# Graph kernel on one core: the third relation's degrees later in the query product, the last product in three fp32r passes

## What is computed

```python
# first layer (three relations): messages are averaged per relation
out = x @ W_root + bias
for r in range(3):
    m = etype == r
    s = segment_sum(where(m, msg, 0), dst); c = segment_sum(m, dst)
    out = out + s / maximum(c, 1.0)[:, None]
# and the gate's query part, one row for each of 8 x 64 queries
qg = einsum('blf,gf->blg', q, Wg[:, F:]) + bg
# last layer (34 relations, then a graph convolution)
mean = agg.reshape(34, n, -1) / maximum(cnt, 1.0)
h1 = einsum('rni,rio->no', mean, W_rel) + x @ W_root + b_rgcn
xw = h1 @ W_gcn                                   # the last product
out = segment_sum(xw[src] * norm[:, None], dst) + xw * (dinv * dinv)[:, None] + b_gcn
```

## Time and profile before

| | us |
|---|---|
| median of 3 runs | 1069.91 |
| lowest, highest | 1068.56, 1072.1 |
| the profiled execution | 1069.65 |
| its span | 1067.8 |
| TensorE busy | 1029.7 |
| VectorE busy | 767.6 |
| ScalarE busy | 574.3 |
| GpSimd busy | 263.5 |

### The profile page before, as it was taken

The page is one execution under the profiler, slowest core; times in us unless marked ns, Lnnn a source line. Parts: engine busy times, 40 slices in busy tenths (PEclk is TensorE's granted clock), DMA queues, the critical chain, the costliest instruction groups (busy, mean ns, idle before and its releaser), DMA issues.

```text
span 1067.8 us, 17748 instructions
## 1 busy us (share of the span) xinstructions
PE 1029.7 (96%) x7444; PEld 853.1 (80%) x7444; DVE 767.6 (72%) x1106; ACT 574.3 (54%) x612; POOL 263.5 (25%) x166
## 2 busy tenths in 40 slices
PE   8999999999999999999899989999999999999997
PEld 6799986454689984445869879967999999999994
DVE  7993855888754237888654495755989898989873
ACT  0433216888633338888324373424767676767650
POOL 3524704899400027988100000000000000000000
PEclk9999999999999999999999999999999999999999
DMA  8033247221042374221335302614978787878740
GB/s 302 12 126 142 90 144 233 63 66 55 6 178 89 119 231 144 60 60 41 109 129 187 125 1 90 214 49 155 302 254 281 256 279 254 280 256 279 255 168 32
DMA packets 82324, 163.20 MB, mean 153 GB/s; under 512 B 4076, under 2 KB 60168, under 8 KB 81950
## 3 DMA queue, kind: packets, MB, share of 16 engines
q1 hardware_dynamic: 80768, 151.86, 42.0%
q0 software_dynamic: 1472, 10.15, 3.4%
HBM read 158.35 MB, written 0.80 MB: 149 GB/s over the span
## 4 chain that ended last, share of the span: by engine, by line
PE 81%; DVE 11%; issue 3%; ACT 2%; DMA 1%; POOL 0%; SPq 0%; DVEq 0%; ACTq 0%
PE PS L1139 20%; PE PS L803 8%; PE PS L974 7%; PE PS L819 6%; PE PS L602 5%; PE PS L701 5%; PE PS L1122 5%; PE PS L725 4%; PE PS L532 4%; PE PS L621 3%; PE PS L545 3%; PE PS L1155 2%; PE PS L1041 2%; DVE PRD L1756 2%; PE PS L861 2%
## 5 line engine op out<-in xcount | busy, mean ns | idle before, releaser
L2025 DVE TENSOR_TENSOR Wlo<-W,Whi 128x2304 fp32r<-128x2304 f32 x68 | 172.1, 2550 | 18.9 <-ACT Whi L1496 18.9
L1496 ACT CAST Whi<-W 128x2304 fp32r<-128x2304 f32 x68 | 144.4, 2126 | 0.0
L1139 PE MATMUL PS<-Whi,Mhi 128*128 128x384 f32 x408 | 138.1, 338 | 0.0
L1139 PE MATMUL PS<-Wlo,Mhi 128*128 128x384 f32 x408 | 136.6, 335 | 0.0
L1139 PE MATMUL PS<-Whi,Mlo 128*128 128x384 f32 x408 | 136.5, 335 | 0.0
L499 POOL TENSOR_TENSOR PRDP<-arena 128x1024 f32<-128x1024 f32 x48 | 114.7, 2390 | 33.0 <-issue 20.6
L803 PE MATMUL PS<-QH,SEL 128*128 128x512 f32 x384 | 115.8, 422 | 5.9 <-DVE PRD L1756 1.5
L1338 ACT ACTIVATE arena<-PS 128x1024 f32<-128x1024 f32 x96 | 98.5, 1026 | 24.2 <-PE PS L803 24.2
L803 PEld LDWEIGHTS PS<-QH,SEL 128*128 128x128 f32 x384 | 64.8, 188 | 55.8 <-DVE PRD L1756 21.5
L1338 ACT ACTIVATE PS<-PS 128x1024 f32<-128x1024 f32 x96 | 98.0, 1021 | 2.6 <-PE PS L803 2.6
L1139 PEld LDWEIGHTS PS<-Whi,Mhi 128*128 128x128 f32 x408 | 76.9, 188 | 0.4 <-DVE Wlo L2025 0.2
(11 more groups left out here) (306 smaller groups left out, 2421.1 us busy)
## 6 DMA issues: line engine op xcount, KB each, us to landing
W<-in_L_rel SPq DMA_DIRECT2D x68, 1152.0 KB, 6.5
W<-in_W_rel SPq DMA_DIRECT2D x6, 2304.0 KB, 9.2
W<-in_W SPq DMA_DIRECT2D x6, 2304.0 KB, 9.1
arena<-in_qU SPq DMA_DIRECT2D x96, 128.0 KB, 2.7
W<-in_WqT SPq DMA_DIRECT2D x4, 2304.0 KB, 8.7
W<-in_W_root SPq DMA_DIRECT2D x2, 2304.0 KB, 13.3
W<-in_WgT SPq DMA_DIRECT2D x2, 2304.0 KB, 8.5
QH<-QH POOLq DMA_DIRECT2D x2, 1536.0 KB, 9.7
```

The costliest lines, as they stand in the source:

```text
L1139: mm = pe.matmul(PS[:, 4 + s % 2, 0:HALF], MS[a][mb][:, k, j * P:(j + 1) * P], WS[b][w % 3][:, k, :], start=n == 0, stop=n == 17)
L1496: nc.scalar.copy(WS[0][w % 3][:], W[(FIRST34 + r) % 2][:, :, q * HALF:(q + 1) * HALF]).then_inc(w_hi, 1)
L2025: V.tensor_tensor(WS[1][w % 3][:], W[(FIRST34 + r) % 2][:, :, q * HALF:(q + 1) * HALF], WS[0][w % 3][:].bitcast(F32), ALU.subtract).then_i ...
```

## The change

In the first stage the spreading of the third relation's degrees moves from between the tiles to behind two of the second tile's three thirds. In the last layer the weights `L3_gcn` become members 68 and 69 of the ring: SyncE loads them by halves, ScalarE and VectorE split them as the others, and the sums are split in high and low part (`MS`) in place of the copies to hT. The last product runs 18 fp32r matmuls for each of its four quarters: high x high, low x high, high x low. The other branch keeps the plain product and reads the weights by halves.

```diff
-            for n in range(2 * R34):
+            for n in range(2 * R34 + 2):
...
-                sp.dma_start(W[(FIRST34 + r) % 2][:, :, cols], turned(A["L3_rel"][r])[:, :, cols]).then_inc(rel_w_in[r % 2][q], 16)
-            m = FIRST34 + R34
-            sp.wait_ge(w_lo, 2 * R34 - 2)
-            sp.dma_start(W[m % 2][:], turned(A["L3_gcn"])).then_inc(w_in[m % 2], 16)
+                source = A["L3_rel"][r] if r < R34 else A["L3_gcn"]
+                sp.dma_start(W[(FIRST34 + r) % 2][:, :, cols], turned(source)[:, :, cols]).then_inc(rel_w_in[r % 2][q], 16)
...
             natural3(qT[1], W[0], bank=3, tiles=[0])
+            natural3(qT[1], W[0], bank=3, last=True, tiles=[1], thirds=[0, 1])
             spread_counts(2, CNT[:, 2], bank=7)
-            natural3(qT[1], W[0], bank=3, last=True, tiles=[1]).then_inc(w_used, 1)
+            natural3(qT[1], W[0], bank=3, last=True, tiles=[1], thirds=[2]).then_inc(w_used, 1)
...
+                for t, h in product(range(NT), range(2)):
+                    if (t, h) != (0, 0):
+                        mm.then_inc(rows_done, 1)
+                    w = 2 * R34 + h
+                    pe.wait_ge(w_hi, w + 1)
+                    for a, b in ((0, 0), (1, 0), (0, 1)):
+                        if b:
+                            pe.wait_ge(w_lo, w + 1)
+                        for k in range(KC):
+                            if t == h == b == 0 and k % 2 == 0:
+                                if a:
+                                    pe.wait_ge(gcn_dve, 1 + k // 2 + 1)
+                                else:
+                                    pe.wait_ge(gcn_act, 2 + k // 2 + 1)
+                            mm = pe.matmul(PS[:, 2 * t + h, 0:HALF], MS[a][1][:, k, t * P:(t + 1) * P], WS[b][w % 3][:, k, :],
+                                           start=a == b == k == 0, stop=b == 1 and k == KC - 1)
+                mm.then_inc(w_used, 1)
...
             def weight_hi(w):
-                if w >= 2 * R34:
+                if w >= 2 * R34 + 2:
                     return
...
+                for i in range(3):
+                    act.wait_ge(gcn_sum, 3 + i + 1)
+                    nc.scalar.copy(MS[0][1][:, 2 * i:2 * i + 2, :], PS[:, sums_bank(2) + i, :].rearrange("p (k n) -> p k n", k=2)
+                                   ).then_inc(gcn_act, 1)
...
             def weight_lo(w):
-                if w >= 2 * R34:
-                    return
...
-                middle_sums(2)
+                if split:
+                    weight_lo(2 * R34 + 1)
+                    for i in range(3):
+                        dve.wait_ge(gcn_act, 2 + i + 1)
+                        V.tensor_tensor(MS[1][1][:, 2 * i:2 * i + 2, :], PS[:, sums_bank(2) + i, :].rearrange("p (k n) -> p k n", k=2),
+                                        MS[0][1][:, 2 * i:2 * i + 2, :].bitcast(F32), ALU.subtract).then_inc(gcn_dve, 1)
+                else:
+                    middle_sums(2)
                 gcn_out(2, 0)
```

More of the change, by code:

```diff
@@ L1157, in scatter, with last_product @@
                 return mm
-            def last_product():
+            def last_product(split):
                 keep_busy(10, 7)
                 gcn_sums(2)
-                m = FIRST34 + R34
-                pe.wait_ge(w_in[m % 2], 16 * (FIRST34 // 2 + 1))
-                natural(0, hT, W[m % 2], ready=sums_ready(2), half_sem=rows_done).then_inc(w_used, 1)
+                if not split:
+                    for q in range(2):
+                        pe.wait_ge(rel_w_in[R34 % 2][q], 16 * (R34 // 2 + 1))
+                    natural(0, hT, W[(FIRST34 + R34) % 2], ready=sums_ready(2), half_sem=rows_done).then_inc(w_used, 1)
+                    return
+                for t, h in product(range(NT), range(2)):
[15 more added lines that the diff above has]
+                mm.then_inc(w_used, 1)
             overflow = pe.value_load(flag[0:1, 0:1])
@@ L1190, in _ @@
                 scatter(PAIRS34 - 1, (3,)).then_inc(enc_done, 1)
-                last_product()
+                last_product(True)
             with pe.Else():
@@ L1221, in _ @@
                 pe.sem_inc(enc_done, 1)
-                last_product()
+                last_product(False)
         @block.scalar
@@ L1559, in _ @@
                 relation(R34 - 1, 1, nxt=False)
-            sums_out(2)
+                sums_out(2)
             norm_x(4)
@@ L2083, in normalise34, with last_rows @@
                 V.tensor_tensor(N34[j], A34[j], RC[:, 1, :].unsqueeze(1).to_broadcast([P, NT, NODES]), ALU.mult).then_inc(nrm_ready, 1)
-            def last_rows():
+            def last_rows(split):
                 dve.wait_ge(w_used, FIRST34)
@@ L2139, in _ @@
                 rows_lo(2 * R34 - 1)
-                last_rows()
+                last_rows(True)
             steps[0] = before
@@ L2151, in _ @@
                 normalise34(R34 - 1, 1)
-                last_rows()
+                last_rows(False)
 _IN = {
```

## The result

The changed kernel takes 1080.28 us in the median (1076.57 to 1080.71), the kernel before 1070.95 over the runs of the same session; the ratio is 1.0082, 95% interval 1.0053 to 1.0112. It is slower. The profiled execution of the changed kernel is its fastest, 1076.57 with a span of 1074.8; the one before was 1069.65 and 1067.8. The other three executions of the changed kernel took 1080.25 to 1080.71. Their mean granted clock was 0.989 against 0.992 in the fastest, and 0.003 of 1075 us are 3.2 of the 3.7 us between them; where in the kernel they lost it no profile shows.

What follows compares the result with a forecast made beforehand. VectorE's row up to the first Tlo, which TensorE meets next, was taken to decide: 1069.65 + 2.65 + 6.7 + 1.7 - 2.9 gives 1077.8 us, 1078.0 for the median; range 1070.9 to 1081.0.

Steps and rivals of the forecast that it cites:

- rival D: Last product gains nothing, as the second half's cast starts late and holds the last row part; 1080.9 us, chance 7%.
- The bound: First stage: VectorE has no slack from the degrees at 53.70 to the first Tlo, which TensorE meets next.
- The lateness: First stage: VectorE gets the third relation's degrees at 56.35 instead of 53.70, 2.65 us lost in full.
- The collision: First stage: VectorE's AI sums overlap GpSimd's two subtractions and wait for both; 6.7 us lost.
- The clock: First stage: TensorE's granted clock falls behind its long wait for the first Tlo; 1.7 us lost, bounds 0 and twice that.
- The last product: End of the kernel: 72 matmuls in 12.48 us replace 15.49 us, added work under cover; 2.9 us gained.
- A: AI sums: VectorE keeps the shared access over the gaps, only lateness and clock remain; 1071.4 us, chance 16%.
- B: AI sums: one gap is lost to GpSimd and not the other, + 4.8; 1074.8 us, chance 12%.
- C: First stage: late degrees cost nothing, TensorE keeps its 3.76 us lead, first Tlo reached by about 74.8; 1063.2 us, chance 5%.

Runs made afterwards that it cites:

- e9: The kernel before with 19 small bf16 matmuls in TensorE's hole ahead of the third relation's degrees; 1069.46 us against 1069.11, ratio 1.0008.
- e10: The changed kernel with the degrees behind one third of tile 1 and GpSimd waiting for the AI sums; 1068.20 us, ratio 0.9989 to the kernel before.
- e3: The changed kernel with GpSimd's subtractions of the second weights waiting until VectorE has finished the AI sums; 1071.62 us, ratio 1.0017 to the kernel before.
- e5: The changed kernel with VectorE's first Tlo parts straight behind the scan, then query parts, AI sums last; 1062.32 us, ratio 0.9938 to the kernel before.
- e7: The changed kernel with the degrees behind one third of tile 1, VectorE's queue as in the change; 1074.47 us, ratio 1.0057 to the kernel before.
- e8: The changed kernel run again, unchanged, beside the others on one chip; 1077.74 us, ratio 1.0079 to the kernel before.
- e4: The changed kernel with 90 small bf16 matmuls, results not used, ahead of the first aggregate; 1077.08 us, ratio 1.0063 to the kernel before.
- e2: The kernel before with only the new last product, the degrees staying between the tiles; 1066.84 us, ratio 0.9971.

## Why the prediction was right, point by point

**The number.** Forecast 1078.0 against a median before of 1069.91, a ratio of 1.0076; measured 1.0082. The time itself, 1080.28, is 2.3 us above the forecast and only 0.7 below the end of the range; 1.0 of it is that the kernel before was slower too in that session (1070.95). By the number alone rival D (1080.9) lies nearest, so the number decides little here. In the profiled execution the forecast was 1.2 too high (1077.8 against 1076.57): 0.6 in the first stage (11.05 against 10.49), 0.3 that came back behind it, 0.45 at the very end, less 0.2 by which the last product gained less than forecast. What speaks for the mechanism is the rows and the runs that follow.

**The bound.** That VectorE's row from the degrees to the first Tlo decides is shown three ways: filling the hole in the kernel before gave nothing (e9), bringing the degrees in time gave 3.0 us (e10 against e3), and moving 9 us of other work behind that Tlo turned the change from 1.008 to 0.994 (e5).

**The lateness.** Forecast 2.65 us; VectorE starts the degrees at 56.15 instead of 53.70, 2.45. The 0.2 are TensorE's, which ran that much earlier in this execution.

**The collision.** Forecast 6.7 us. The AI sums end at 79.95 instead of 71.19, 8.76 late in all, so 6.31 are the collision; taking it away gave 6.6 (e3). The size was right and one detail of the mechanism was not: I had the first sum follow the scan without a gap and keep GpSimd off, and GpSimd's two turns fall before the second and the last sums. The rows show the turns one place earlier, before the first (3.86) and the second (3.79) sum. GpSimd got its turn at the end of the scan although no wait stood there. The number of turns, two, is what set the price, and that it was the same two turns by another order is luck: e7, where I counted the turns by the same reasoning, came out one turn too low.

The Trainium skill ("SBUF — State Buffer", Who interferes with whom) says that a VectorE instruction with two SBUF inputs contends with a GpSimd instruction that reads SBUF, under an exclusive lock. That rule spoke against this change. The runs agree with it: 3.86 us beside GpSimd's subtraction, and 0.67 with the same operands where GpSimd waits (e3) or comes later (the kernel before).

**The clock.** Forecast 1.7 us; 8 records took 3.73 us and took 2.00 before (79.11 to 81.11), so 1.73. The steps sum to 2.45 + 6.31 + 1.73 = 10.49, and the second product starts 91.59 - 81.11 = 10.48 later. The size was right for this execution. In e8 the same hole cost 2.7 (1.78 in the third part, 0.93 in the product behind it), so 1.7 is not a fixed price. That a low clock costs this where TensorE is the bound rests on these records; the run that was to show it in the median (e4) stays open, as its interval overlaps.

**The last product.** Forecast 2.9 us; 2.72 in the profile, 3.1 by the ratio of e2. The first pass waited 0.30 us for ScalarE's third copy, where I had 0.15. The added casts and subtractions lay under cover as said: the last row part is released by TensorE, as before, and follows 0.62 us of idle time on ScalarE where there were 2.62.

**The rivals.** A (VectorE keeps its place) and B (one turn) are excluded by the two long sums, C by the wait of 12.76 us, D by e2. D's end lies near the measured median all the same, and without e2 and the rows the number would not exclude it. C's condition, a first Tlo that comes early enough, is what e5 makes by hand, and it gives C's price: I had 1063.2, a ratio of 0.9937, and measured 0.9938.

**Where I was off** was the use of my own reading. I priced the low clock behind the first hole as something that TensorE gets back, in the expectation of e9, when the row said that it only shortens a wait. And in e7 I trusted the start of one GpSimd instruction to a microsecond.

## What to carry to other kernels

Closing a hole on the busiest engine pays only if what it meets next is ready earlier too: look for the next wait it has on the other engine, here one of 0.29 us, and for what stands in that engine's queue before it. Moving a step back in one queue moves everything behind its wait on the other, so put the piece that others wait for first and the bookkeeping last; that was worth 15 us here, between 1.0079 and 0.9938. The collision was not removed by it (it stands at 85 to 91 in e5), only moved to where TensorE does not wait for it. And an engine that gets ahead starts its helpers earlier, which may then run against instructions they had just missed.

## What the runs showed that I had not expected

The fall of the clock behind the same short hole is not certain. Behind 2.01 us before the degrees it fell in the profile of the kernel before; behind 2.10 us at the same place it did not in e2. Behind 1.85 us at 314 it fell in e8 (and in e2 and e4 at the same wait), and not in the first profile of the changed kernel. What a fall costs depends on what TensorE meets next: nothing behind the hole before the degrees (e9), about 1 us behind the wait at 314 (e8), and 1.7 to 2.9 behind the wait for Tlo, over the seven profiles in which that wait is 2.9 us or more. Most of these kernels' times spread over 1.8 to 6.2 us; the reordered ones, which have no hole in the first stage but still the wait of 1.85 us in the second layer, over 0.7 and 1.1. That the clock makes most of the spread fits this and is not shown, as only one execution of each was profiled.

Two instructions that follow each other on VectorE without a wait may still let GpSimd in between: after the scan it did (3.86 us for the sum behind it), while in the kernel before GpSimd's subtraction of 10.27 us, which lasted through both PROW and PCOL, says that it got no turn between those two. Which instructions hand over and which do not stays open here.
